# Patch embedding in two-part fp32r products, projections issued ahead of exchanges, a table value with a two-step correction in all norms, and two experts summed ahead of their weights

## The reference, cut to what matters

```
h = patches @ W_lin.T + b_lin, class token in front, + positions         # 768 -> 256
n = layernorm(h)
x = n + global_latent_attn(rmsnorm(n, w1))      # 16 heads of 16, latent 64, rope, q/k rms norm
x = x + local_gqa_attn(rmsnorm(x, w2))          # the same with 4 key/value heads, rope
h = h + x
n = layernorm(h)
h = h + moe(n)      # 2 shared units + 32 experts of 128, sigmoid router, 8 of 32, 2 of 4 groups
h = h + attention(layernorm(h))                 # 16 heads, biases
h = h + quantised_mlp(layernorm(h))             # 256 -> 1024 -> 256, 127 levels
...
moe: y_e = (silu(x Wg_e.T) * (x Wu_e.T) * weight_e) @ Wd_e.T, summed over e
rmsnorm(x, w) = x * rsqrt(mean(x*x) + 1e-6) * w
```

## Time and profile before

| | us |
|---|---|
| median of 3 runs (lowest, highest) | 381.12 (379.61, 382.11) |
| profiled execution, own time | 379.39 |
| its span | 377.6 |
| PE busy | 349.9 (93%) |
| DVE busy | 231.7 (61%) |
| ACT busy | 179.4 (48%) |
| POOL busy | 137.5 (36%) |

### The profile page before, as it was taken

The page is one execution under the profiler, slowest core; times in us unless marked ns, Lnnn a source line. Parts: engine busy times, 40 slices in busy tenths (PEclk is TensorE's granted clock), DMA queues, the critical chain, the costliest instruction groups (busy, mean ns, idle before and its releaser), DMA issues.

```text
span 377.6 us, 9798 instructions
## 1 busy us (share of the span) xinstructions
PE 349.9 (93%) x3916; PEld 292.7 (78%) x3916; DVE 231.7 (61%) x495; ACT 179.4 (48%) x353; POOL 137.5 (36%) x144
## 2 busy tenths in 40 slices
PE   8999898899898899999999999999999999889664
PEld 6655665568667899999999999999997788656333
DVE  0265689786879355555555555555554663666686
ACT  0156944487473244444444444444445774224270
POOL 0035852270260266665656544443310013410021
PEclk9999999999999999999999999999999999999899
DMA  8940001000550224444454544545200000000001
GB/s 295 366 144 0 3 6 30 0 3 3 169 169 2 90 97 142 141 146 148 148 147 148 143 139 127 146 133 152 80 1 2 0 2 3 5 3 0 0 2 66
DMA packets 14865, 32.08 MB, mean 85 GB/s; under 512 B 2480, under 2 KB 4464, under 8 KB 14576
## 3 DMA queue, kind: packets, MB, share of 16 engines
q1 hardware_dynamic: 12592, 29.66, 24.8%
q10 hardware_dynamic: 2240, 1.95, 1.5%
HBM read 30.91 MB, written 0.69 MB: 84 GB/s over the span
## 4 chain that ended last, share of the span: by engine, by line
PE 72%; DVE 14%; ACT 5%; DMA 3%; issue 3%; ACTq 1%; DVEq 0%
PE psum L1090 72%; DMA region<-in_w_lin 2%; DVE xn L792 1%; DVE rc L857 1%; DVE nt L786 1%; ACT region L749 1%; DVE nt L788 1%; DVE nt L789 1%; DMA wb<-weights 1%; DVE km L1072 1%; ACT km L584 1%; DVE pk L797 1%; DVE xc L777 1%; ACT sq L562 1%; ACT ars L565 1%
## 5 line engine op out<-in xcount | busy, mean ns | idle before, releaser
L1090 PE MATMUL psum<-xh,split_all 128*128 128x296 f32 x544 | 122.6, 299 | 1.8 <-DVE rt L986 1.8
L464 POOL TENSOR_TENSOR split_all<-km,split_all 128x768 fp32r<-128x768 f32 x34 | 63.7, 1876 | 85.0 <-ACT split_all L670 85.0
L1090 PEld LDWEIGHTS psum<-xh,split_all 128*128 128x128 f32 x544 | 91.7, 188 | 2.3 <-DVE rt L986 2.1
L1090 PE MATMUL psum<-xl,split_all 128*128 128x296 f32 (+1 forms) x288 | 85.1, 300 | 0.2 <-ACT e L641 0.2
L690 ACT ACTIVATE ah<-rt 128x296 fp32r<-128x296 f32 x68 | 30.7, 451 | 78.4 <-DVE rt L986 71.9
L1090 PEld LDWEIGHTS psum<-xl,split_all 128*128 128x128 f32 (+1 forms) x288 | 53.1, 187 | 1.1 <-POOL xl L507 0.4
L988 DVE TENSOR_TENSOR al<-rt,ah 128x296 fp32r<-128x296 f32 x64 | 30.0, 468 | 33.1 <-ACT ah L690 33.1
L1090 PE MATMUL psum<-ah,split_all 128*128 128x296 f32 x272 | 48.4, 300 | 1.3 <-ACT ah L690 1.3
L983 DVE TENSOR_TENSOR rb<-psum,wb 128x296 f32<-128x296 f32 x64 | 29.9, 467 | 31.8 <-ACT psum L688 28.1
L1090 PEld LDWEIGHTS psum<-ah,split_all 128*128 128x128 f32 x272 | 40.6, 188 | 1.8 <-ACT ah L690 1.8
L986 DVE TENSOR_TENSOR rt<-rb,psum 128x296 f32<-128x296 f32 x64 | 29.6, 463 | 5.2
(11 more groups left out here) (176 smaller groups left out, 530.7 us busy)
## 6 DMA issues: line engine op xcount, KB each, us to landing
km<-in_experts SPq DMA_DIRECT2D x34, 384.0 KB, 4.0
wb<-weights SPq DMA_DIRECT2D x32, 296.0 KB, 3.7
w_sb<-in_w SPq DMA_DIRECT2D x2, 1024.0 KB, 11.6
region<-in_x SPq DMA_DIRECT2D x6, 296.0 KB, 5.3
region<-in_w_lin ACTq DMA_DIRECT2D x6, 128.0 KB, 6.3
qkv_sb<-in_qkv_w SPq DMA_DIRECT2D x1, 768.0 KB, 4.7
cst<-in_consts ACTq DMA_DIRECT2D x1, 502.5 KB, 6.4
out<-x SPq DMA_DIRECT2D x2, 148.0 KB, 2.1
```

The source lines that it names most:

```text
L464: nc.gpsimd.tensor_tensor(wl[i], ring[i], wh[i].bitcast(f32), ALU.subtract)\
L1090: return nc.tensor.matmul(out_, lhsT, rhs, start=start, stop=stop, skip_group_check=True)
```

## The change

1. **Patches in parts.** ACT copies each weight slice and each half of a patch slice to fp32r (the high part), DVE subtracts for the low parts, into one of three slots in the space of the experts' parts; PE sums 12 products a slice in place of 4 in fp32. All six weight slices are loaded ahead of the constants.
2. **Projection order.** PE's iteration u is now: project u+1, exchange u, head mean of u. Projections use three banks in turn (4, 6, 2), and the value sums' banks are swapped.
3. **Norms.** ACT squares the table value; DVE has two steps: t=(v+eps)y², t=(t-3)y. The result is -2 times what it was (or POOL's weighting carries the -0.5), and the consumers take a factor -0.5.
4. **Experts.** The two shared products stand earlier in DVE's router. PE sums gate and up of units 2 and 3, both halves, before the first routed down sum; DVE makes silu times up for them first (`early`) and multiplies by the weights after.

```diff
@@ ScalarE, start @@
-            for k in range(LEAD):
+            for k in range(KT):
                 act_e.dma_start(w_lin_sb[:, k, :], w_lin[:, k, :]).then_inc(s_x[k], 16)
             act_e.dma_start(cst[:], consts).then_inc(s_cst, 16)
             act_e.dma_start(vec[:], vecs).then_inc(s_cst, 16)
             act_e.dma_start(nt[:, 0:NBF], consts_bf).then_inc(s_cst, 16)
-            for k in range(LEAD, KT):
-                act_e.dma_start(w_lin_sb[:, k, :], w_lin[:, k, :]).then_inc(s_x[k], 16)
             act_e.dma_start(down_sb[:], g_down).then_inc(s_attn_w[0], 16)
             act_e.dma_start(gk_sb[:], g_k).then_inc(s_attn_w[0], 16)
             act_e.dma_start(gv_sb[:], g_v).then_inc(s_attn_w[0], 16)
+            for k in range(KT):
+                i = k % PATCH_SLOTS
+                act_e.wait_ge(s_x[k], 32)
+                if k >= PATCH_SLOTS:
+                    act_e.wait_ge(s_pmm, k - PATCH_SLOTS + 1)
+                nc.scalar.activation(pw_hi[i], w_lin_sb[:, k, :], ACT.Copy).then_inc(s_pwh, 1)
+                for hf in range(2):
+                    nc.scalar.activation(px_hi[i][:, half(hf)], patches[:, k, half(hf)], ACT.Copy).then_inc(s_pxh, 1)
...
@@ VectorE, start @@
+            for k in range(KT):
+                i = k % PATCH_SLOTS
+                dve.wait_ge(s_pwh, k + 1)
+                nc.vector.tensor_tensor(pw_lo[i], w_lin_sb[:, k, :], pw_hi[i].bitcast(f32), ALU.subtract).then_inc(s_pwl, 1)
+                for hf in range(2):
+                    dve.wait_ge(s_pxh, 2 * k + hf + 1)
+                    nc.vector.tensor_tensor(px_lo[i][:, half(hf)], patches[:, k, half(hf)],
+                                            px_hi[i][:, half(hf)].bitcast(f32), ALU.subtract).then_inc(s_pxl, 1)
...
@@ TensorE, start @@
             for k in range(KT):
-                pe.wait_ge(s_x[k], 32)
+                i = k % PATCH_SLOTS
+                pe.wait_ge(s_pwh, k + 1)
+                for hf in range(2):
+                    pe.wait_ge(s_pxh, 2 * k + hf + 1)
+                    for c in range(C):
+                        mm(ps[2 * c + hf][:, 0:HALF], pw_hi[i][:, c * P:(c + 1) * P], px_hi[i][:, half(hf)], k == 0, False)
+                pe.wait_ge(s_pwl, k + 1)
                 for hf in range(2):
                     for c in range(C):
-                        ins = mm(ps[2 * c + hf][:, 0:HALF], w_lin_sb[:, k, c * P:(c + 1) * P],
-                                 patches[:, k, half(hf)], k == 0, k == KT - 1)
+                        mm(ps[2 * c + hf][:, 0:HALF], pw_lo[i][:, c * P:(c + 1) * P], px_hi[i][:, half(hf)], False, False)
+                    pe.wait_ge(s_pxl, 2 * k + hf + 1)
+                    for c in range(C):
+                        ins = mm(ps[2 * c + hf][:, 0:HALF], pw_hi[i][:, c * P:(c + 1) * P], px_lo[i][:, half(hf)],
+                                 False, k == KT - 1)
...
@@ norms: ScalarE, then VectorE @@
-                    nc.scalar.activation(ars[:, half(hf)], ps[2 + hf][:, 0:HALF], ACT.Abs_reciprocal_sqrt,
-                                         bias=eps[:, eps_at:eps_at + 1]).then_inc(s_ars, 1)
+                    link(nc.scalar.activation(ars[:, half(hf)], ps[2 + hf][:, 0:HALF], ACT.Abs_reciprocal_sqrt,
+                                              bias=eps[:, eps_at:eps_at + 1]))
+                    nc.scalar.activation(nt[:, half(hf)], ars[:, half(hf)], ACT.Square).then_inc(s_ars, 1)
...
-                    link(nc.vector.scalar_tensor_tensor(t, ps[2 + hf][:, 0:HALF], eps[:, eps_at:eps_at + 1], y,
+                    link(nc.vector.scalar_tensor_tensor(t, ps[2 + hf][:, 0:HALF], eps[:, eps_at:eps_at + 1], t,
                                                         ALU.add, ALU.mult))
-                    link(nc.vector.scalar_tensor_tensor(t, t, -0.5 * factor, y, ALU.mult, ALU.mult))
-                    link(nc.vector.scalar_tensor_tensor(t, t, 1.5 * factor, y, ALU.add, ALU.mult))
+                    link(nc.vector.scalar_tensor_tensor(t, t, -3.0, y, ALU.add, ALU.mult))
...
@@ TensorE, projections @@
             def qk_units(a):
...
+                projection(a, 0)
+                for u in range(NPROJ):
+                    if a == 0 and u < 2:
+                        latent_sums(u)
+                    if u + 1 < NPROJ:
+                        projection(a, u + 1)
+                    exchange(a, u)
+                    head_mean_squares(a, u)
...
@@ VectorE, router @@
             link(ins)
+            shared_product(0, 0)
             link(nc.vector.tensor_tensor(gsum[:], top[:, :, :, 0], top[:, :, :, 1], ALU.add))
...
-            shared_product(0, 0)
             link(nc.vector.tensor_scalar(masked[:], masked[:], 0.0, None, ALU.add))
             for t in range(TT):
                 ins = nc.vector.max(top[:, t, 0, :], masked[:, t, :])
             link(ins)
+            shared_product(1, 1)
             for t in range(TT):
                 ins = nc.vector.match_replace(repl[:, t, :], top[:, t, 0, :], masked[:, t, :], -3.0e38)
             link(ins)
-            shared_product(1, 1)
...
@@ VectorE, units 2 and 3 @@
+            early = (gu, qcopy)
+            for u in range(SHARED, NRING):
+                for j in range(2):
+                    n = 2 * u + j
+                    dve.wait_ge(s_sg, n + 1)
+                    dve.wait_ge(s_u, n + 1)
+                    nc.vector.tensor_tensor(early[u - SHARED][:, j, :], sg[:, j, :], ps[5 + 2 * j][:, 0:HALF], ALU.mult)\
+                        .then_inc(s_mulc, 1)
             for u in range(SHARED, NRING):
                 dve.wait_ge(s_wb[u], 16)
                 for j in range(2):
-                    expert_unit(2 * u + j, j, ps[6 + j][:, 0:HALF], wb[:, u, half(j)])
+                    n = 2 * u + j
+                    dve.wait_ge(s_mulc, n - 2 * SHARED + 1)
+                    if u > SHARED:
+                        dve.wait_ge(s_al, n - 2 * SHARED - 1)
+                    nc.vector.tensor_tensor(act[:, j, :], early[u - SHARED][:, j, :], wb[:, u, half(j)], ALU.mult)\
+                        .then_inc(s_act, 1)
+                for j in range(2):
+                    n = 2 * u + j
+                    dve.wait_ge(s_ah, n + 1)
+                    if u > SHARED:
+                        dve.wait_ge(s_down, n - 1)
+                    nc.vector.tensor_tensor(al[:, j, :], act[:, j, :], ah[:, j, :].bitcast(f32), ALU.subtract)\
+                        .then_inc(s_al, 1)
...
@@ ScalarE, units 2 and 3 @@
             for i in range(SHARED, NRING):
-                expert_unit(2 * i, 0, ps[6][:, 0:HALF])
+                for j in range(2):
+                    n = 2 * i + j
+                    act_e.wait_ge(s_g, n + 1)
+                    if i > SHARED:
+                        act_e.wait_ge(s_mulc, n - 2 * SHARED - 1)
+                    nc.scalar.activation(sg[:, j, :], ps[4 + 2 * j][:, 0:HALF], ACT.Silu).then_inc(s_sg, 1)
                 high_part(i + AHEAD, (i + AHEAD) % NRING, (i + AHEAD) // NRING)
-                expert_unit(2 * i + 1, 1, ps[7][:, 0:HALF])
+            for i in range(SHARED, NRING):
+                for j in range(2):
+                    n = 2 * i + j
+                    act_e.wait_ge(s_act, n + 1)
+                    if i > SHARED:
+                        act_e.wait_ge(s_down, n - 1)
+                    nc.scalar.activation(ah[:, j, :], act[:, j, :], ACT.Copy).then_inc(s_ah, 1)
...
@@ TensorE, units 2 and 3 @@
-            for u in (2, 3):
-                up_sums(u, u, 1)
-                down_sums(u, u, 0)
-                up_sums(u + 1, (u + 1) % NRING, 0)
-                down_sums(u, u, 1)
+            up_sums(2, 2, 1, 6, 4)
+            up_sums(3, 3, 0, 4, 5, 1)
+            up_sums(3, 3, 1, 6, 6, 2)
+            down_sums(2, 2, 0)
+            down_sums(2, 2, 1)
+            down_sums(3, 3, 0)
+            up_sums(4, 0, 0, 4, 7, 3)
+            down_sums(3, 3, 1)
```

More of the change, by code:

```diff
@@ L179, in program @@
         pairs_r = split_all[:, 0:P]
+        PW = 2 * (T + D)
+        pslot = [split_all[:, i * PW:(i + 1) * PW] for i in range(PATCH_SLOTS)]
+        px_hi, px_lo = [s_[:, 0:T] for s_ in pslot], [s_[:, T:2 * T] for s_ in pslot]
+        pw_hi, pw_lo = [s_[:, 2 * T:2 * T + D] for s_ in pslot], [s_[:, 2 * T + D:PW] for s_ in pslot]
         wb_flat = wb[:].rearrange("p r t -> p (r t)")
@@ L416, in norm_weighted @@
                         ins = nc.gpsimd.tensor_scalar(xn[:, c, half(hf)], src[:, c, half(hf)],
-                                                      weight[:, c:c + 1], 0.0, ALU.mult, ALU.add)
+                                                      weight[:, c:c + 1], -0.5 * factor, ALU.mult, ALU.mult)
                     ins.then_inc(s_xw, 1)
@@ L678, in _ @@
                 act_e.wait_ge(s_xn, 4 + hf + 1)
-                nc.scalar.activation(xh[:, :, half(hf)], xn[:, :, half(hf)], ACT.Copy).then_inc(s_xh, 1)
+                nc.scalar.activation(xh[:, :, half(hf)], xn[:, :, half(hf)], ACT.Copy, scale=-0.5).then_inc(s_xh, 1)
```

(26 more changed lines are left out.)

98 lines of the change are left out of this document (46 added, 52 removed).

## The result

The change made the kernel slower: 384.91 us median of 20 runs (381.11 to 388.25) beside 380.53 (378.77 to 384.37) for the kernel before. The ratio is 1.0081, 95% interval 1.0054 to 1.0107, which is +3.1 us (+2.1 to +4.1); it leaves out disturbed executions, so it is smaller than the distance of the two medians. The forecast was 380.4 and its range ended at 383.6: wrong in sign and outside the range. The profiled execution took 386.84 (span 385.1), 7.5 more than the one of before, so it is slower than most runs of the changed kernel, and its shifts are read one by one here, not as a total.

What follows compares the result with a forecast made beforehand. The chain that ended last lay 72% on TensorE, with the experts' 150 of 378 us immovable. Terms +3.2-0.9-1.7-1.0-0.3+0 = -0.7 us took 381.1 to 380.4 (chance 0.50), range 377.0 to 383.6.

Steps and rivals of the forecast that it cites:

- part 4: Router and seam ahead of the experts: early sums change nothing, 0 us, bounds -0.2 and +0.3.
- The chain of three: Seam ahead of the experts: PE waits for product, weighting and ACT's high part, 1.55 us, instead of the weights' DMA.
- Rival (c): Seam: early sums fill PE's wait of 1.84 us, won on top of (a); -4.2, 376.9 us; chance 0.08.
- Part 1: Patch embedding at the start: PE starts and ends later, clock lost behind the idle gap; +3.2 us.
- the clock's term: Start: some 3.7 us at 1.2 GHz behind PE's idle gap lose 1.7 us, bounds 0 and 1.7.
- (b): Start: no table load for Copy, PE starts at 7.9 and the clock likely stays; -3.7, 377.4 us; chance 0.08.
- (a): Start: PE's clock survives the idle gap, 1.7 us less; -2.4, 378.7 us; chance 0.17.
- (d): Start: the clock, once lost, stays at 1.2 GHz through the whole embedding; +5.7, 386.8 us; chance 0.07.
- Part 2: Two projection stages: projection ahead of exchange gains 1.7 us in the first stage and 0.9 in the second.
- rival (e): Projections are bound by ACT and DVE anyway, so part 2 brings 0; 383.0 us; chance 0.10.
- Part 3: Norms: DVE's second half is a step, 0.50 us, shorter, counting ahead of the router and in the last norm; -1.0.
- an even chance of 0.3: Last norm: the shorter gap may keep the clock full, first feed-forward chunk 0.6 us earlier; even chance, counted -0.3.

Runs made afterwards that it cites:

- part 4 alone: The kernel before with only the early sums and the earlier shared products; +0.3 us (-0.9 to +1.5) against the kernel before.
- the run with the high parts earlier: The changed kernel with ScalarE's high parts of units 4 and 5 one step earlier; -1.0 us (-2.2 to +0.2) against the kernel before.
- the old router: The changed kernel, high parts one step earlier, shared products back at their old places in VectorE's router; -1.3 us (-2.4 to -0.3) against the kernel before.
- part 1 alone: The kernel before with only the patches in parts; +3.9 us (+2.4 to +5.3) against the kernel before.
- part 2 alone: The kernel before with only the new projection order; -0.8 us (-1.8 to +0.3) against the kernel before.
- part 3 alone: The kernel before with only the changed norms; -2.0 us (-3.2 to -0.8) against the kernel before.
- the early start: Six transfers of constants and attention weights issued by SP, not ACT; with parts 1, 2 and 3, -5.2 us (-6.7 to -3.8) against the kernel before.
- parts 2 and 3 together: The kernel before with the projection order and the norms, without parts 1 and 4; -3.3 us (-4.7 to -1.9) against the kernel before.
- the ten filling products: The changed kernel with ten products of constants on PE before the first routed down sum; +1.2 us (+0.2 to +2.3) against the kernel before.
- the fastest kernel: Parts 1 to 3, transfers on SP, early sums, high parts one step earlier, shared products at old places; 374.83 us, -7.1 against the kernel before.

## Why the prediction was wrong

The step that failed is **part 4**, "0, bounds -0.2 and +0.3". It should have been +2.3, as the change stands in the whole (+3.1 with it, +0.8 without; the intervals leave some 1.7 either way), and the trace of part 4 alone has 2.2: 0.8 for the router (0.68 and 0.39 longer beside POOL, less the 0.26 of the row shown below), 1.0 for the seam's waits, the rest behind them. The chain of three was right and so was the order of DVE's program; what failed is the 0.48 for the weighting, which took 2.09. The DVE operations of the experts that the trace of before has beside POOL read PSUM, and they keep their length there:

```profile
153.12 1.85 POOL L464 TENSOR_TENSOR split_all<-km,split_all 128x768 fp32r<-128x768 f32 x1 [1.86 <-ACT split_all L670]
153.37 0.47 DVE L983 TENSOR_TENSOR rb<-psum,wb 128x296 f32<-128x296 f32 x1 [0.58 <-ACT psum L688]
```

The early sums change just this: the product is made first and the weighting reads two tiles in SBUF. The bound of +0.3 left out the one engine not in the chain, and the router's 0.8 was put at nothing ("earlier shared sums win no time") where they lose some. Nothing in the trace of before shows a DVE operation held for 2 us, but it has a small one, in the router:

```profile
123.32 0.82 POOL L470 TENSOR_TENSOR al<-rt,ah 128x296 fp32r<-128x296 f32 x1 [1.36 <-ACT ah L690]
123.75 0.43 DVE L969 TENSOR_SCALAR wsum<-wsum 128x5 f32<-128x5 f32 x1
```

It ends 0.04 behind POOL. In the changed kernel, where POOL rests at that place (126.44), the same operation takes 0.17. The Trainium skill ("GPSIMD Engine Reference", Specifications) says that POOL shares its SBUF interfaces with VectorE and that DVE instructions with two SBUF inputs contend with it. The traces agree: `rt<-rb,wb` has two such inputs and took 2.09 us in place of 0.455, while the product of 137.70 in the run with the high parts earlier, which reads PSUM, took its 0.46 in the middle of POOL's 1.85. It speaks against this change, and the prediction did not weigh it.

Rival (c), early sums that fill the wait, was held to fail because of the order of DVE's program. It fails for POOL. With POOL moved it is partly true, and only with the old router: 0.5 to 0.7 by the traces.

**Part 1**, +3.2: mechanism right, size 0.7 short (+3.9, and +3.7 in the trace). PE's start at 9.38 was right to 0.2. The low clock lasted 5.3 us in part 1 alone and cost 2.3 to 2.4, not 1.7; in the two profiles of the changed kernel the 72 records took 1.7 and 2.6 more than the 10.05 at full pace, so in the first the clock's term was right and the rest, 2.0 in place of 1.5, was short. The table load for the Copy came, so (b) is out; (a) and (d) did not come about either: the pace was low behind the gap and came back. The sign "a granted clock under 1 somewhere from 9 to 13" can't be read from the clock's row of the first profile, only from the records. The value was 1.7 at the upper of two bounds, and the bound was no bound.

**Part 2**: second stage -0.9, seen -1.06 in the changed kernel (14.99 us from its first projection to its table load, 16.05 before). First stage -1.7, seen -0.6 (17.36, 17.93 before). With part 2 alone the exchanges stand so:

```profile
28.77 0.66 PE L1090 MATMUL psum<-qcopy,cst 128*128 128x296 f32 x2
...
31.00 0.76 PE L1090 MATMUL psum<-latent,gk_sb 64*128 64x296 f32 x2
31.70 0.77 PE L1090 MATMUL psum<-qcopy,cst 128*128 128x296 f32 x2
32.30 0.66 PE L1090 MATMUL psum<-sq,cst 128*128 128x296 f32 x2
...
36.00 0.66 PE L1090 MATMUL psum<-qcopy,cst 128*128 128x296 f32 x2
36.50 0.66 PE L1090 MATMUL psum<-sq,cst 128*128 128x296 f32 x2
```

Exchange 3 was put at 34.5 from a projection 0 at 25.16; it came at 36.00 from one at 25.37. PE reads busy from end to end, and 36 records took 10.63 us: 0.295 each, not 0.26. Most of it lies at the latents, whose operands have 64 rows or columns: from 31.00 two records take 0.70, the two of the exchange behind them 0.60, while the exchange at 36.00, away from them, takes 0.50. A wait for ScalarE inside the spans is about 0.3 in all, at 33.9. The term counted all records at one pace, and the trace of before had the other: four latent records from 27.59 to 28.73, 0.285 each. Measured in all, -0.8 (-1.8 to +0.3) against -2.6 said; rival (e), 0, is inside that interval.

**Part 3**: -1.0 and an even chance of 0.3; measured -2.0 (-3.2 to -0.8). The gap ahead of the last peak is as foreseen, to 0.03 us (2.85 said; the earlier trace rows has 3.35); part 3 alone:

```profile
350.72 0.39 PE L1091 MATMUL psum<-cst,pk 128*1 128x128 f32 x2 [2.82 <-DVE pk L1046]
```

and norm 2's stretch (its table load to the silu load) fell from 10.6 and 10.5 to 10.0. Behind that gap the clock held in the two profiles with the early start and parts 2 and 3, and fell in all others, so the chance of one half was too high for this kernel. What else is in the 2.0 is not settled.

**The sum**: said +3.2-2.6-1.3+0=-0.7. Measured +3.9-3.3 (parts 2 and 3 together) +2.3 = +2.9, beside +3.1 for the whole. The sum is off by 3.6: part 4 by 2.3, part 1 by 0.7, parts 2 and 3 by 0.6 (alone, part 2 was 1.8 short and part 3 0.7 over). By the ratio the change is 0.8% slower, inside the 1% that was given 0.70, and still outside the range: on the slow side the range had only (e) behind it, and the miss came from a part that was given no rival of its own there.

**Left open**: part 4 alone measured +0.3 (at most +1.5), which by itself does not contradict the recorded 0, and its trace has +2.2; that trace took 382.93, 1.6 above its median, and the runs' mean granted clock was 0.988 beside 0.984 before, which is in its favour. The 2.3 rests on the changed kernel with and without the part. And why the clock fell in the router and at the seam in some profiles with no early sums, and what makes the pace of 890 records.

## What to carry to other kernels

When work is moved on one engine, look at what every other engine does at its new place, above all a long GpSimd instruction beside VectorE operations that have both inputs in SBUF: price them to the end of the GpSimd instruction, and move that if it can be moved. A change that turns a PSUM input into one in SBUF brings an operation into this class. An idle stretch of TensorE can cost more than its length, if the clock falls behind it. Where the clock's row matters, check it against the distance of the records, and compare stretches of two profiles only after their paces. A pace read in one stage holds for records of the same shapes; read it in the very stage.

## What the runs showed of the hardware

- A VectorE operation with two SBUF inputs that starts beside a GpSimd two-input operation is held to its end: 2.09 us for 0.455, 0.92 for 0.24, 0.71 for 0.32. Started 0.05 us ahead of it, it takes its usual time. With an input in PSUM it keeps its 0.47 inside GpSimd's 1.85. A small operation with one SBUF input, `wsum<-wsum`, was held too, 0.43 for 0.17.
- At the seam a single wait of 3.12 us was followed by a granted clock of 0.50 in both profiles; waits of 1.48 and 1.09 with work between were not. Length alone does not decide: it fell behind 1.82 with the ten filling products ahead, behind 1.78, 1.80, 1.84 and 2.64 in kernels without early sums that had lost it in the router before, and not behind 1.82, 1.84, 2.00, 2.02 and 2.15 in others.
- At the start, 4.35 us of idleness came before a granted 0.50, 0.75 and 0.63 before full pace. In the fastest kernel's profile 0.88 came before records 0.247 apart until 9.9, so here too the length does not decide.
- Ahead of its first entry a profile's clock reads 1.00 whatever the records do: six a us from 10 to 13 in the changed kernel, at a first entry of 13.3.
- At the same granted clock of 1.00 three profiles had 890 records in 120 us of the experts, the other fifteen 884 or 883.
- The first Copy brought a table load, 1.28 us, and the copy started at its end (8.48 behind 7.19+1.28).
- When the experts' first weights land moves norm 2 by up to 1.8 us between two profiles of one kernel.
